# Layer 1's feed-forward on one core: four of its eight chunks as 23 blocks of routed rows

## The chip, the cores and the metric

The kernel is one program on one core of a Trainium2 chip. The metric is device microseconds of one execution: 2776.56 us before, the median of three runs (2775.31 to 2779.29). The profile shown is one further execution of the same program, which took 2766.23 us in all, 2764.4 us of it the span of the trace.

## The reference

Four layers run in sequence over an activation `x` of 4096 tokens (16 samples of 256) by 128 channels. Each has an attention and a feed-forward, each behind a LayerNorm with a shift and scale per sample, and each is added back after a gate per sample:

```
h = layernorm(x) * (1 + ca) + sa;  x = x + ga * attention(h)
h = layernorm(x) * (1 + cb) + sb;  x = x + gb * feedforward(h)
```

In layer 1 the feed-forward holds a second, narrow attention (16 heads of 8 channels), a LayerNorm that makes `x1`, and a mixture of 8 experts of which each token takes two:

```
x1 = ln(h + attention(h))
gates = softmax(x1 @ gW + gb);  w = the two largest gates, the others 0
y[e]  = relu(x1 @ W1[e] + b1[e]) @ W2[e] + b2[e]        128 -> 256 -> 128
ff = ln(x1 + sum over e of w[e] * y[e])
```

All of it is float32. A token's result from the six experts that it does not take is multiplied by zero, so these need not be computed. Layer 0's feed-forward is a similar mixture (top two of 8, with a product of two projections), layer 2 has a narrow causal attention and 16 small experts, layer 3 closes.

## The kernel before

`X` stays in on-chip memory as 32 tiles of 128 tokens; a chunk is 4 tiles, so there are 8 chunks. Every stage is a set of functions, one for each engine (`tensor`, `vector`, `scalar`, `gpsimd`, `sync`), that run over the same numbered steps `t`; the order on an engine is the order in which its function issues. Engines meet at semaphores alone. A stage hosts the last steps of the one before it (`tail`) and the first steps of the next (`guest`), so that stages overlap. There is no planner: the tables of pieces by step are written by hand. Banks of the on-chip accumulators are handed out in rings (`m` 2 banks, `g` 4, `y` 2), and each use waits for the reader of the use before it.

- **Layer 1's mixture** is `moe(1, 8, X1)` (`moe` begins at line 1962). It runs 64 dense units: 8 chunks times 8 experts. A unit of step `t` is `tensor_up` (two products of 128 x 512, float32), ScalarE's two Relu, and, two steps later, `tensor_down` (eight products of 128 x 128) and VectorE's `vector_down` (line 2358): four operations that multiply by the gate and add to the accumulator `ACC`. For each chunk the pieces `x1` (four transposes), `logits`, `gate` (softmax and `keep_top2`), `spread` and `seed` (the bias of the second layer times the gates) stand beside the units. After a chunk's last unit, `gpsimd_finish` and `vector_finish` do the LayerNorm (GpSimd adds `x1`, scales and shifts with `LNW` at lines 2495 and 2497; VectorE subtracts and multiplies at 2383), and the gated residual (lines 171 and 174). The stage's last such finish is hosted by the next stage.
- **Layer 0's mixture** is `routed_experts()` and works otherwise: chunks 0 and 3 are 16 dense units, the six others are routed. VectorE finds the two experts of each token, TensorE ranks them (`rank`), and VectorE makes a row address for each pair of token and expert. GpSimd then writes each tile twice to the array `hs` in device memory by an indirect DMA (line 1853: 48 of them, 128 rows each). Then 31 blocks of 256 rows follow, each with one expert: SyncE reads the row address and the weight address from tables, loads 256 rows (line 1890) and 900 columns of weights (line 1897), TensorE transposes the rows (line 1431), runs the up and down products, and SyncE stores the result in order (line 1902). Weights have four buffers, rows three. In the next stage, wide attention of layer 1, GpSimd gathers each token's two results (line 1209, `late_fetch`) and combines them (`late_combine`).
- **Narrow attention 2** (`narrow_attention(2)`, layer 2) follows layer 1's mixture. It has 128 steps, one for each pair of heads and samples, with a row maximum on VectorE in each (line 3014), and pieces for chunk c from step 16(c - 2) + 2. Its queries and keys go to device memory and back through SyncE (`Parts`, lines 2685 and 2694). It starts as a guest from step 55 of the 64 of layer 1's mixture.
- **Wide attention 0** clears `hs` from device memory, 10 DMAs of 1472 KB on SyncE's queue.

Of the kernel before, what the change touches and what calls it, by code (L numbers as in the profile page):

```python
# [8 lines left out]
F32 = mybir.dt.float32  # L9
F16 = mybir.dt.float16  # L10
BF16 = mybir.dt.bfloat16
# [72 lines left out]
def program(nc, dr, out, stages=STAGES):  # L84
    ctx = ExitStack()
    with ctx:
# [55 lines left out]
        ld_x = [sem(f"ld_x{k}") for k in range(8)]  # L142
# [55 lines left out]
        class Norm:  # L198
# [17 lines left out]
            def stats(self, e, c, i0=0, i1=4):  # L216
                if self.c0 == 0:
                    e.wait_ge(ld_x[c], 16)
                elif i0 == 0:
                    self.arrived(e, c)  # L220
# [61 lines left out]
        def start_up():  # L282
            def sync(e):
                e.dma_start(CT, dr["c0"]).then_inc(ld_wm, 16)
                e.dma_start(WM, dr["wmod0"]).then_inc(ld_wm, 16)
                for k in range(8):
                    e.dma_start(X[:, 4 * k:4 * k + 4, :], dr["x"][:, 4 * k:4 * k + 4, :]).then_inc(ld_x[k], 16)
# [20 lines left out]
        modulation_own = Own(sem("modulation_v"))  # L308

        class Modulation:  # L310
# [3 lines left out]
            def __init__(self, k, sc, gr, tmp):  # L314
                self.k, self.sc, self.gr, self.tmp = k, sc, gr, tmp
                self.own = modulation_own
# [108 lines left out]
        wide_own = Own(sem("wide_v")), Own(sem("wide_g"))  # L425

        def wide_attention(layer, opening=None):
# [14 lines left out]
            own_v, own_g = wide_own  # L442
# [625 lines left out]
            def sync(e):  # L1068
# [4 lines left out]
                for b in range(16):  # L1073
# [13 lines left out]
                    if causal and 2 <= b < 12:  # L1087
                        part = slice(2944 * (b - 2), 2944 * (b - 1))
                        e.dma_start(dr["hs"].rearrange("(p n) c -> p (n c)", p=128)[:, part], dr["zero"]).then_inc(st_zero, 16)
                    if not causal and b == 8:  # L1090
# [50 lines left out]
        moe_own = Own(sem("moe_v")), Own(sem("moe_g"))  # L1141
# [43 lines left out]
        y_stored = [sem(f"y_stored{i}") for i in range(2)]  # L1185
        place(21736)
# [9 lines left out]
        NBLK, SLOT_ROWS = 31, 3072  # L1196

# [14 lines left out]
        def late_combine(e, n):  # L1212

            own, tile = wide_own[1], 8 + n
# [12 lines left out]
        def routed_experts():  # L1227
# [11 lines left out]
            own, own_g = moe_own  # L1239
            scattered, marked, spaced, share_exped = sem("scattered"), sem("marked"), sem("spaced"), sem("share_exped")  # L1240
            placed, table_made = sem("placed"), sem("table_made")
            rows_in = [sem(f"rows_in{i}") for i in range(3)]
            weights_in = [sem(f"weights_in{i}") for i in range(4)]
# [598 lines left out]
            def gpsimd_scatter(e, m):  # L1842
# [3 lines left out]
                if m == 0:  # L1846
                    e.wait_ge(st_zero, 160)
# [113 lines left out]

        def moe(k, E, X1=None):
# [6 lines left out]
            own, own_g = moe_own  # L1969
# [658 lines left out]
        X1A = alloc(4096)  # L2628
# [18 lines left out]
        narrow_own = Own(sem("narrow_v")), Own(sem("narrow_g"))  # L2647
# [93 lines left out]
        def narrow_attention(k):  # L2741
# [9 lines left out]
            own, own_g = narrow_own  # L2751
            causal = k == 2
            X1a = X1A.rearrange("p (t c) -> p t c", c=128)
# [37 lines left out]
            norm = Norm(own, own_g, MODS[k % 2], 2 if k == 1 else 0, slots, r0)  # L2791
# [16 lines left out]
            def hosted_step(i):  # L2808

                if k == 1:  # L2810
# [6 lines left out]
                        [(1, "split"), (1, "v"), (1, "turn")]][i]  # L2817

# [291 lines left out]
            def vector(e):  # L3110
                pads_vector(e, False)
                for t in range(last + 1):
                    if t < 128:
                        rowmax(e, t)
                    if t:
                        for step, b in posts(t - 1):
                            vector_post(e, step, b)
# [1029 lines left out]
```

## Time and profile before

| what | value |
|---|---|
| median of three runs | 2776.56 us |
| the profiled execution | 2766.23 us, its span 2764.4 us |
| TensorE busy | 2608.0 us, 94% |
| VectorE busy | 2017.9 us, 73% |
| ScalarE busy | 1665.9 us, 60% |
| GpSimd busy | 1183.3 us, 43% |
| mean granted TensorE clock | 0.985 |

Times in the rows are microseconds from the span's start. A row of a line in the timeline gives start, duration, engine, line, operation, output and input, the number of operations merged in it, and in brackets how long the engine was idle before it and what ended that. A busy TensorE is not TensorE at its peak: products are pipelined and their ends are modelled. Stages by time: wide attention 0 to about 610, layer 0's mixture to about 880 (its blocks 762 to 855), wide attention 1 to about 1480, narrow attention 1 to 1753, layer 1's mixture to 2012, narrow attention 2 to about 2260, then layers 2 and 3.

### The profile page before, as it was taken

The page shows a single profiled execution, that of the slowest core. Times are in us where ns is not written, and L with a number is a line of the kernel's source. Part 1 is how long each engine was busy: PE and PEld are TensorE (multiplying, and loading weights), DVE is VectorE, ACT ScalarE, POOL GpSimd, SP SyncE. Part 2 cuts the span into 40 slices and gives each one's busy share as a digit, 9 for nine tenths or more (in the row PEclk, how much of TensorE's full clock was granted, in tenths as well). Part 3 has the DMA queues.
Part 4 walks back from the last instruction along what each step waited for, and adds up shares of the span by engine and source line. Part 5 has one row for each costly group of instructions (what it writes and reads, how often), then busy time and mean ns, then how long its engine had stood idle before and what let it go on. Part 6 is the DMA issues. An engine that isn't in the chain of part 4 may idle for free.

```text
span 2764.4 us, 67999 instructions
## 1 busy us (share of the span) xinstructions
PE 2608.0 (94%) x24870; PEld 1786.7 (65%) x24870; DVE 2017.9 (73%) x5620; ACT 1665.9 (60%) x4107; POOL 1183.3 (43%) x1620
## 2 busy tenths in 40 slices
PE   6999999998999999999997999999989989999898
PEld 2666666666687666666664555677767755666676
DVE  6988888876644666676666998466678885887675
ACT  3888888885335766777764777443335544334665
POOL 6888888863602565111124454122333321014441
PEclk9999999999999999999999999999999999999999
DMA  3022221212374111121115543000054433435750
GB/s 114 17 54 76 77 75 48 68 33 82 131 230 129 37 41 42 32 48 32 24 25 145 164 135 122 1 14 3 29 162 140 126 92 63 93 79 158 205 166 28
DMA packets 218857, 230.81 MB, mean 83 GB/s; under 512 B 18608, under 2 KB 188272, under 8 KB 216480
## 3 DMA queue, kind: packets, MB, share of 16 engines
q1 hardware_dynamic: 212000, 207.58, 27.2%
q10 hardware_dynamic: 3456, 12.58, 1.4%
q0 software_dynamic: 3072, 6.30, 0.8%
q8 instruction: 201, 3.29, 0.5%
q14 instruction: 128, 1.05, 0.1%
HBM read 165.87 MB, written 75.60 MB: 87 GB/s over the span
## 4 chain that ended last, share of the span: by engine, by line
PE 73%; DVE 12%; ACT 7%; issue 4%; POOL 2%; DMA 1%; SPq 1%; ACTq 0%; DVEq 0%; POOLq 0%
PE pb L163 65%; ACT big L967 4%; PE pb L663 3%; ACT big L160 2%; DVE big L3014 2%; DVE big L837 2%; PE pb L596 2%; DVE big L236 1%; DVE big L3519 1%; PE pb L2985 1%; PE pb L249 1%; DVE big L820 1%; DVE big L747 1%; POOL hs L1853 1%; DVE big L842 0%
## 5 line engine op out<-in xcount | busy, mean ns | idle before, releaser
L163 PE MATMUL pb<-big 128*128 128x128 f32 (+12 forms) x19624 | 2345.0, 327 | 94.2 <-ACT big L160 32.4
L163 PEld LDWEIGHTS pb<-big 64*128 64x128 bf16 (+4 forms) x19624 | 1476.5, 143 | 750.8 <-issue 422.6
L160 ACT ACTIVATE big<-pb 128x512 f32<-128x512 f32 (+7 forms) x1481 | 846.3, 620 | 541.0 <-PE pb L163 293.0
L160 ACT ACTIVATE big<-pb,big 128x512 f32<-128x512 f32 (+2 forms) x502 | 276.6, 586 | 406.7 <-PE pb L163 356.1
L3014 DVE TENSOR_REDUCE big<-pb 128x4 f32<-128x1024 f32 (+1 forms) x256 | 277.6, 1086 | 71.4 <-PE pb L163 66.8
L967 ACT ACTIVATE big<-big 128x256 f32<-128x256 f32 x512 | 254.0, 499 | 69.5 <-DVE big L842 68.2
L967 ACT ACTIVATE big<-pb,big 128x128 f32<-128x128 f32 (+1 forms) x512 | 257.1, 527 | 60.3 <-DVE big L822 60.1
L837 DVE CUSTOM_DVE_ANT_0 big<-pb,big 128x256 f32<-128x256 f32 x512 | 186.7, 422 | 96.9 <-PE pb L163 96.7
L187 POOL TENSOR_SCALAR big<-big 128x4 f32<-128x4 f32 (+2 forms) x102 | 26.8, 263 | 533.7 <-DVE big L182 533.6
L174 POOL TENSOR_TENSOR big<-big 128x128 f32<-128x128 f32 x168 | 74.8, 459 | 340.8 <-DVE big L171 340.7
L1046 POOL TENSOR_TENSOR big<-big 128x512 f32<-128x512 f32 x128 | 159.9, 1277 | 141.6 <-DMA big<-recip 141.5
L663 PEld LDWEIGHTS pb<-big 64*128 64x128 f32 x3584 | 145.7, 138 | 72.4 <-ACT big L967 55.8
L663 PE MATMUL pb<-big 64*128 64x64 f32 x3584 | 157.7, 225 | 24.0 <-ACT big L967 23.1
L1020 POOL TENSOR_TENSOR big<-big 128x32 f32<-128x32 f32 x32 | 174.1, 5441 | 2.7
L747 DVE TENSOR_TENSOR big<-pb,big 128x512 f32<-128x512 f32 x256 | 163.9, 681 | 13.2 <-PE pb L163 11.7
L904 DVE COPY big<-pb 128x384 f32<-128x384 f32 (+1 forms) x256 | 157.1, 613 | 2.9 <-PE pb L663 1.9
L2358 DVE SCALAR_TENSOR_TENSOR big<-pb,big 128x128 f32<-128x128 f32 x256 | 71.9, 344 | 95.7 <-PE pb L163 95.7
L1011 POOL TENSOR_TENSOR big<-big 128x256 f32<-128x256 f32 x128 | 82.7, 646 | 85.4 <-DVE big L747 82.2
L596 PEld LDWEIGHTS pb<-big 128*128 128x128 f32 x512 | 64.0, 143 | 75.0 <-issue 65.3
L967 ACT ACTIVATION_READ_ACCUMULATOR big<-pb,big 128x1 f32 x512 | 111.3, 217 | 0.0
L236 DVE TENSOR_SCALAR big<-big 128x128 f32<-128x128 f32 x244 | 97.2, 451 | 8.2 <-POOL big L189 8.1
L2737 POOL CAST big<-big 128x16 bf16<-128x16 f32 x96 | 21.9, 228 | 189.1 <-DVE big L3018 73.4
(211 smaller groups left out, 2454.0 us busy)
## 6 DMA issues: line engine op xcount, KB each, us to landing
parts<-big SPq DMA_DIRECT2D x384, 96.0 KB, 2.4
big<-parts SPq DMA_DIRECT2D x72, 512.0 KB, 4.1
big<-recip SPq DMA_DIRECT2D x128, 256.0 KB, 4.9
big<-comb SPq DMA_DIRECT2D x32, 512.0 KB, 8.2
hs<-in_zero SPq DMA_DIRECT2D x10, 1472.0 KB, 8.7
big<-in_wx SPq DMA_DIRECT2D x31, 450.0 KB, 4.4
parts<-big SPq DMA_DIRECT2D x192, 64.0 KB, 2.1
big<-parts ACTq DMA_DIRECT2D x24, 512.0 KB, 4.7
```

What stands on the lines that cost most here:

```text
L160: return e.activation(o, i, f, bias=bias, scale=scale)
L163: return e.matmul(o, l, r_, start=start, stop=stop, skip_group_check=True)
L236: t = e.tensor_scalar(XN[:, i, :], X[:, self.tiles(c)[i], :], mv[:, k0 + i, 0:1], rs[:, k0 + i:k0 + i + 1], ALU.subtract, ALU.mult)
L596: t = e.transpose(bk[:, 128 * m:128 * m + 128], QR[(8 * b + n) % 12][:, 128 * m:128 * m + 128], IDF)
L663: t = e.transpose(banks[2 * (p % 2) + half][:, 64 * at:64 * at + 64], PS[p % 2][rows, i, 128 * blk:128 * blk + 128], IDF[rows, rows])
L747: t = e.tensor_tensor(h3(D), h3(bk), TAB[:, 2 * qk + kk, tile, :].unsqueeze(1).to_broadcast([128, 8, 64]), ALU.mult)
L837: t = e.tensor_tensor_reduce(ps[:, i, x], banks[2 * (p % 2) + i][:, x], U[:, 2 * j + i, 128 - 128 * qt:384 - 128 * qt], 1.0, -3.0e38, ALU. ...
L904: e.tensor_copy(*turned_out(t - 1, 0)).then_inc(even_out, 1)
L967: t = e.activation(ps, banks[2 * s + i][:, at:at + w] if causal else ps, ACT.Exp, bias=NM[s][:, m:m + 1], scale=rstd_q(b)[:, qt, h:h + 1] ...
L1020: e.tensor_tensor(half, half, HALF, ALU.pow).then_inc(rms_made, 1)
L1046: e.tensor_tensor(OT[k % 6], OT[k % 6], R[:, 2 * i:2 * i + 2, :], ALU.mult).then_inc(chunk_scaled, 1)
L3014: e.tensor_reduce(m[:, :, 0:n, jj], two[:, :, 0:width].rearrange("p e (q x) -> p e q x", q=n), AXX, ALU.max, negate=True).then_inc(maxed, 1)
```

## The change

`moe(1, 8, X1)` is replaced by `routed_ffn()`. Chunks 0, 1, 6 and 7 stay dense (units 0 to 15 at steps 0 to 15, units 16 to 31 at steps 39 to 54), chunks 2 to 5 are routed in 23 blocks at steps 16 to 38.

- `X1` gets 130 columns a tile: two more words carry, for each token, the row of its result and the number of its second expert. Routing is done in two groups of two chunks; its pieces stand in the last steps of narrow attention 1 and beside the first 16 units. GpSimd scatters 32 times (128 rows of 520 bytes) into `hs1`, three in a step, at steps 2 to 7 and 8 to 13.
- A block loads 256 rows of `hs1` and 642 columns of weights, has one up product where layer 0 has two, and ends in two indirect DMAs from GpSimd that scatter the results to `ys1` (`SPOT` is their row, worked out by VectorE from the two words).
- A token's two results then lie side by side. SyncE loads them as 8 half chunks (`late_fetch_rows`), and each half (2 tiles) is finished in steps: sum and LayerNorm statistics on VectorE, `late_rstd` on GpSimd, `late_normed` on ScalarE, then scale, shift and gate and the residual. Four halves stand beside the dense units of chunks 6 and 7, scaled and gated by VectorE (`late_scale_vector`); four more, and the four halves of chunks 6 and 7 themselves, stand at steps 8 to 56 of narrow attention 2, with GpSimd doing scale, gate and residual.
- Dense chunks 0 and 1 are finished by VectorE but for the residual. The guest of narrow attention 2 starts at step 48 of 55.
- Wide attention 0 also fills `hs1`: 9 DMAs of 1040 KB. The load of layer 2's second gates moves from block 5 to block 11 of narrow attention 2. Semaphores are shared or renamed (`vector_own`, `gpsimd_own`, `ld_rows`).

```diff
+            DENSE, ROUTED = (0, 1, 6, 7), (2, 3, 4, 5)
+            NB1 = 23
+            T0, T1 = 16, 16 + NB1
+            T = T1 + 16
+            modulated_at, guests_at = T1 + 1, T - 7
+            scatters = {t: [(m, three[m % 3]) for m in range(3 * (t - first), min(3 * (t - first) + 3, 16))]
+                        for first in (2, 8) for t in range(first, first + 6)}
+            summed_at = {T1 + 3: 0, T1 + 4: 1, T1 + 6: 2, T1 + 7: 3}
+            finishes = {10: (0, 1), 12: (0, 2), 13: (0, 3), 18: (1, 1), 20: (1, 2), 21: (1, 3)}
...
+            def tensor_block_up(e, j):
+                s, J = slots["rows", j], NBLK + j
+                e.wait_ge(s.free, s.n)
+                e.wait_ge(weights_in[J % 4], 16 * (J // 4 + 1))
+                s = slots["g", T0 + j]
+                bk = fill(e, s)
+                for f in range(2):
+                    t = mm(e, bk[:, 256 * f:256 * f + 256], WB[J % 4][:, 128 * f:128 * f + 128], HTB[J % 3], True, True)
+                t.then_inc(s.full, 1)
...
+            def vector_block_down(e, j):
+                y, J = slots["y", T0 + j], NBLK + j
+                bk = empty(e, y)
+                if j >= 4:
+                    e.wait_ge(y_placed[j % 4], 32 * (j // 4))
...
+            def scalar(e):
+                for t in range(T + 2):
...
+                        scalar_block_up(e, t - T0)
+                    if T0 <= t + 1 < T1:
+                        scalar_rows(e, t + 1 - T0)
...
+            def gpsimd_block_out(e, j):
+                y = slots["y", T0 + j]
+                e.wait_ge(y.free, y.n)
+                for i in range(2):
+                    e.indirect_dma_start(out=dr["ys1"], out_offset=bass.IndirectOffsetOnAxis(ap=SPOT[j % 4][:, i:i + 1], axis=0),
+                                         in_=YB[j % 4][:, i, :], in_offset=None).then_inc(y_placed[j % 4], 16)
...
+            def sync_weights(e, j):
+                J = NBLK + j
+                if j >= 4:
+                    y = slots["y", T0 + j - 4]
+                    e.wait_ge(y.free, y.n)
...
+        def late_sum(e, i, k):
...
+            for j in range(2):
+                a, n = CHOSEN1[buffer][:, j, :, :], 2 * i + j
+                x = e.scalar_tensor_tensor(out=a[:, 0, :], in0=a[:, k, :], scalar=SHARE1[:, k, n:n + 1],
+                                           in1=a[:, 0, :] if k else X1[:, 8 + n, 0:128], op0=ALU.mult, op1=ALU.add)
...
+                return [(i, t - first) for i, first in zip(range(4, 12), range(8, 56, 6)) if 0 <= t - first < 7]
...
-                 moe(1, 8, X1A.rearrange("p (t c) -> p t c", c=128)), narrow_attention(2), moe(2, 16), layer3_attention(), layer3_mix()]
+                 routed_ffn(), narrow_attention(2), moe(2, 16), layer3_attention(), layer3_mix()]
```

## Rows read from the trace of the kernel before

**Rows 1.** The page: busy time by engine.
```profile
PE 2608.0 (94%) x24870; PEld 1786.7 (65%) x24870; DVE 2017.9 (73%) x5620; ACT 1665.9 (60%) x4107; POOL 1183.3 (43%) x1620
```
**Rows 2.** Busy time by engine in layer 1's mixture; last clock, DMA share, GB/s.
```profile
1753.00:1813.00 60.00, 59.95 (x354) 44.21 (x353) 32.35 (x114) 23.22 (x37) 10.31 (x20) 1.00 0.00 1
```
**Rows 3.** Timeline of VectorE, line 2358, five units in a row.
```profile
1779.94 1.13 DVE L2358 SCALAR_TENSOR_TENSOR big<-pb,big 128x128 f32<-128x128 f32 x4 [2.23 <-PE pb L163]
...
1784.72 1.12 DVE L2358 SCALAR_TENSOR_TENSOR big<-pb,big 128x128 f32<-128x128 f32 x4 [3.01 <-PE pb L163]
...
1788.66 1.13 DVE L2358 SCALAR_TENSOR_TENSOR big<-pb,big 128x128 f32<-128x128 f32 x4 [2.81 <-PE pb L163]
...
1793.06 1.13 DVE L2358 SCALAR_TENSOR_TENSOR big<-pb,big 128x128 f32<-128x128 f32 x4 [2.69 <-PE pb L163]
...
1796.56 1.13 DVE L2358 SCALAR_TENSOR_TENSOR big<-pb,big 128x128 f32<-128x128 f32 x4 [1.18 <-PE pb L163]
```
**Rows 4.** Timeline of one of layer 0's blocks, all engines.
```profile
798.59 0.84 ACT L160 ACTIVATE big<-pb,big 128x256 f32<-128x256 f32 x2 [1.37 <-PE pb L163]
...
799.25 0.38 PE L1431 MATMUL pb<-big 128*128 128x128 f32 x2
...
799.47 2.79 PE L163 MATMUL pb<-big 128*128 128x128 f32 x16
...
799.67 0.39 ACT L160 ACTIVATE big<-pb 128x256 f32<-128x256 f32 x1 [0.24 <-PE pb L1431]
...
800.56 0.42 DVE L1705 TENSOR_TENSOR big<-pb,big 128x256 f32<-128x256 f32 x1 [0.18 <-PE pb L163]
...
801.44 0.35 SPq L1897 DMA_DIRECT2D big<-in_wx  x1
...
802.09 0.38 PE L1431 MATMUL pb<-big 128*128 128x128 f32 x2
```
**Rows 5.** GpSimd's scatter at line 1853: one in the timeline, then all 48 (min/median/max ns).
```profile
739.97 0.96 POOL L1853 DMA_INDIRECT hs<-big  x1 [0.31 <-issue]
...
L1853 POOL DMA_INDIRECT hs<-big x48: 955/962/1248, 683.1 to 755.2; - x48
...
DMA to landing us min/median/max: 2.2/2.2/5.6
```
**Rows 6.** Landing of the 31 weight loads of line 1897.
```profile
DMA to landing us min/median/max: 3.4/4.4/5.8
```
**Rows 7.** Stretches with and without pauses of TensorE; columns as in rows 2.
```profile
795.00:815.00 20.00, 19.73 (x126) 17.71 (x124) 9.95 (x24) 8.59 (x21) 0.00 (x0) 1.00 0.85 236
815.00:820.00 5.00, 2.41 (x11) 1.88 (x12) 1.30 (x3) 0.84 (x2) 0.00 (x0) 0.98 1.11 292
820.00:825.00 5.00, 5.00 (x26) 4.48 (x25) 1.06 (x3) 1.61 (x4) 0.00 (x0) 0.68 0.76 206
615.00:630.00 15.00, 11.88 (x148) 7.90 (x142) 12.59 (x45) 13.42 (x46) 4.36 (x6) 1.00 0.43 95
```
**Rows 8.** VectorE's line 236 without and beside GpSimd's work.
```profile
1973.73 1.11 DVE L236 TENSOR_SCALAR big<-big 128x128 f32<-128x128 f32 x4
...
1988.36 3.91 DVE L236 TENSOR_SCALAR big<-big 128x128 f32<-128x128 f32 x4
```
**Rows 9.** Timeline: narrow attention 2's first split, its reload, and its early scores.
```profile
1990.40 0.61 POOL L2663 CAST big<-big 128x512 bf16<-128x512 f32 x1
...
2000.44 0.81 SPq L2694 DMA_DIRECT2D big<-parts  x2
...
2012.65 0.56 PE L163 MATMUL pb<-big 64*128 64x256 bf16 x8 [1.44 <-DVE big L3014]
```
**Rows 10.** Narrow attention 2, fill and steady part; columns as in rows 2.
```profile
2012.00:2044.00 32.00, 25.47 (x306) 16.70 (x308) 25.92 (x58) 8.60 (x14) 14.40 (x27) 0.79 0.45 153
2044.00:2094.00 50.00, 48.80 (x772) 35.67 (x768) 40.40 (x83) 27.07 (x42) 17.76 (x34) 1.00 0.54 164
```

**Rows 11.** A stretch in which `hs` is cleared; columns as in rows 2.
```profile
300.00:350.00 50.00, 49.38 (x462) 32.21 (x459) 44.07 (x86) 41.80 (x130) 41.16 (x42) 1.00 0.24 79
```

More of the change, by code:

```diff
@@ L217, in stats @@
                 if self.c0 == 0:
[L218 removed]
+                    e.wait_ge(ld_rows[c], 16)
                 elif i0 == 0:
@@ L1238, in routed_experts @@
             T = TD + NBLK
[L1239 to L1243, printed above, removed]
+            own, own_g = vector_own, gpsimd_own
             some = lambda n: [alloc(512) for _ in range(n)]
@@ new lines, in late_stats @@
+        def late_stats(e, i):
+            own, rows = vector_own, late_rows(i)
+            if i >= 8:
+                e.wait_ge(dense_summed[i // 2 - 2].free, dense_summed[i // 2 - 2].n)
+            else:
+                e.wait_ge(own.sem, own.n)
+            if i >= 2:
+                e.wait_ge(ffn_rstd, i - 1)
+            for j in range(2):
+                x = e.bn_stats(LST[i % 2][:, j, :], rows[:, j, :])
+            x.then_inc(own.sem, own.up())
+            e.wait_ge(own.sem, own.n)
+            for j in range(2):
+                x = e.bn_aggr(LMV[i % 2][:, j, :], LST[i % 2][:, j, :])
+            x.then_inc(ffn_mean, 1)
@@ new lines, in late_normed, with late_scale_vector @@
+        def late_normed(e, i):
+            e.wait_ge(ffn_rstd, i + 1)
+            for j in range(2):
+                a = late_rows(i)[:, j, :]
+                x = act(e, a, a, ACT.Identity, LNMR[i % 2][:, j:j + 1], LRS[i % 2][:, j:j + 1])
+            x.then_inc(ffn_normed, 1)
+        def late_scale_vector(e, i):
+            own, a, b = vector_own, late_rows(i), 4 + i
+            two = lambda w: w.unsqueeze(1).to_broadcast([128, 2, 128])
+            e.wait_ge(ffn_normed, i + 1)
+            e.tensor_tensor(a, a, two(LNW[:, 256:384]), ALU.mult).then_inc(own.sem, own.up())
+            e.wait_ge(own.sem, own.n)
+            e.tensor_tensor(a, a, two(LNW[:, 384:512]), ALU.add).then_inc(own.sem, own.up())
+            e.wait_ge(own.sem, own.n)
+            e.tensor_tensor(a, a, two(GA[:, b, 128:256]), ALU.mult).then_inc(ffn_scaled, 1)
@@ new lines, in late_scale @@
+        def late_scale(e, i, part):
+            own, a, b = gpsimd_own, late_rows(i), 4 + i
+            two = lambda w: w.unsqueeze(1).to_broadcast([128, 2, 128])
+            if part == 0:
+                e.wait_ge(ffn_normed, i + 1)
+            elif i < 4:
+                e.wait_ge(ffn_scaled, i + 1)
+            else:
+                e.wait_ge(own.sem, own.n)
+            if part == 3:
+                e.tensor_tensor(X[:, 2 * b:2 * b + 2, :], X[:, 2 * b:2 * b + 2, :], a, ALU.add).then_inc(ffn_added, 1)
+            else:
+                w, op = ((LNW[:, 256:384], ALU.mult), (LNW[:, 384:512], ALU.add), (GA[:, b, 128:256], ALU.mult))[part]
+                e.tensor_tensor(a, a, two(w), op).then_inc(own.sem, own.up())
@@ L3117, in vector @@
                             vector_post(e, step, b)
+                        for i, step in late_at(t - 1):
+                            if step < 2 and i < 8:
+                                late_sum(e, i, step)
+                            elif step == 2:
+                                late_stats(e, i)
                         for b, piece in steps(t - 1):
@@ L3181, in scalar @@
                         scalar_post(e, step, b)
+                    for i, step in late_at(t):
+                        if step == 4:
+                            late_normed(e, i)
                     for b, piece in steps(t):
```

701 lines of the change are left out of this document (676 added, 25 removed).

## The prediction

> **What bounds the kernel now.** I read the page first, for the one engine that is busy nearly throughout: TensorE, 2608.0 us, 94% of the span [rows 1]. Then the busy time by stage, to see whether that holds where the change is made: in layer 1's mixture TensorE is busy 59.95 of 60 us at full clock, VectorE 32.35, ScalarE 23.22, GpSimd 10.31, and the DMA engines move 1 GB/s [rows 2]. So this stage (1753 to 2012, 259 us) lasts as long as its products, and what is taken from TensorE there is gained until another engine or a load becomes the limit. Last the timeline, for the price of a unit and for how a block of layer 0 runs.
>
> **What is removed.** VectorE waits for TensorE before each unit, so its starts give TensorE's pace [rows 3]. A unit with nothing beside it takes 3.50 us (1793.06 to 1796.56). The other gaps hold one piece each: 4.78 for `seed` (1.28), 3.94 for `x1` (0.44), 4.40 for `logits` (0.90); `spread` is four transposes as `x1` is, and I take 0.44 for it too. Together 3.06 a chunk. The stage before is then 64 x 3.50 = 224, seven chunks' pieces 21.4, and 13.6 left for the modulation, the guest and the two closing steps; sum 259.
>
> **What stands in its place.** Three stretches.
>
> 1. Units 0 to 15: 56.0. Beside them stand x1 or its like for four chunks (1.8), logits for four (3.6), spread and seed for chunk 1 (1.7), and two rankings of some ten small products, for which I take 1.0 each as an estimate from the 1.28 of `seed`, which is eight. 65.1 us.
>
> 2. The 23 blocks. Here the limit has to be found, and there are five candidates. (a) TensorE: in rows 4 a block of layer 0 is 2.84 (799.25 to 802.09) with TensorE never idle: 0.22 for the transposes (799.25 to 799.47), 2.62 for six quarter units (four up, two down). The new block has four of the six: 1.75 + 0.22 = 1.97. (b) ScalarE's chain: in layer 0 the second up product (0.87) runs while ScalarE reads the first; now there is none. Both Relu wait for the up products, and the copy of the next rows stands behind them on ScalarE, and the next up product waits for that copy: 0.2 to start, 0.84 for two, 0.39 for the copy, some 0.06 to hand over, then 0.87 for the products [rows 4]: 2.36. (c) The four weight buffers: the load for block j+4 waits until VectorE has emptied block j, and TensorE wants it two blocks after its own end of block j. VectorE starts 0.18 after TensorE and takes 0.42, SyncE issues 0.46 later (800.98 to 801.44) [rows 4], the load lands 3.4 to 4.4 later [rows 6], and is now 71% of the size. Half of 4.5 to 5.5 is 2.25 to 2.75. (d) GpSimd: a scatter is 0.96 and 0.31 before the next [rows 5], two in a block are 2.54. Four result buffers allow GpSimd to fall behind, so that 2.54 sets the pace only in the long run. (e) The DMA engines: in layer 0 they are 85% busy over 2.84 us [rows 7] for 450 + 128 + 128 KB; now 321 + 130 + 128 KB is 82%, so some 2.0. No candidate reaches 2.84, and three lie between 2.3 and 2.75. I take 2.6, as they meet on the same waits: 59.8 us. Beside the blocks stand pieces of 4.8 us on TensorE, which has 0.6 idle a block and hides most, and on VectorE the finish of chunk 1 (steps 18 to 21) and the top two of chunk 7 (step 27), each a few us that delay the emptying on which (c) and (d) hang: 4.0 for both. 63.8 us; bounds 54 (2.36 and nothing beside it) and 71 (2.84 and six).
>
> 3. Units 16 to 31: 56.0 and the same 13.6 as before: 69.6.
>
> The sum is 198.5 against 259: 60.5 us less.
>
> **What it costs elsewhere.** The last steps of narrow attention 1 get two more turns and logits (2.7 us of TensorE, which has pauses there) and routing on VectorE: +2, bounds 0 and 4. At the first block, 32 scatters at 1.27 with two small jobs leave GpSimd about 2 us behind its three a step; a landing of 2.2 [rows 5] and the load of rows, which I take to land like a weight load, 4.4 [rows 6], follow: +1.5, bounds 0 and 5. In units 18 to 25 VectorE has 1.13 for the unit and about 4.0 for a half (four sums at the 0.28 of rows 3, four small statistics that I put at 0.28 too, three scalings of 128 x 256 at the 0.42 of line 1705 in rows 4, and hand-overs), in 3.50 us: it is full, but the sums begin three units after the last block, when results have landed (two scatters 2.5, landing 2.2, load 4.4). +2, bounds 0 and 6. The guest starts two units nearer the end. Its first split stands 22.2 us ahead of the scores, of which 14.5 are the trip of queries and keys through device memory (10.0 to the reload's issue, and a landing that I take at 4.4 again), so two units (7.0) just fit: 0 to 2, and against it VectorE no longer has the last finish (about 5 us) in the fill of narrow attention 2, where TensorE is busy 25.47 of 32 us and waits for VectorE [rows 9, 10]: together 0, bounds -4 and +2. In the steady part VectorE has 9.6 free of 50 us [rows 10]; eight halves add about 2.5 us each for four and 1.1 each for four within 80 us, and GpSimd's part, four operations of 128 x 256 that I put at 0.61 each [rows 9] and a root, 3 to 4 each, stands beside 17.76 of 50: +2, bounds 0 and 6. Moving the load of second gates and renaming semaphores: nothing, since neither is waited for. The nine fills of `hs1` are like the clearing of `hs`, beside which TensorE is busy 49.38 of 50 us [rows 11]: 0, bounds 0 and 2. Sum +7.5.
>
> So -53 us. The profiled execution, 2766.2 (span 2764.4), becomes 2713; the median of the runs lies 10.3 above it, and I carry the difference over to it: 2776.6 - 53 = **2723.5**.
>
> **Two rules weighed.** Line 236 takes 1.11 us alone and 3.91 beside GpSimd's operations [rows 8], while the 48 scatters keep 955 to 1248 ns, median 962, with VectorE at work beside them [rows 5]. The Trainium skill ("SBUF — State Buffer", section "Who interferes with whom") has VectorE's two-port modes and GpSimd exclude each other, and its section "SBUF: two separate sides" has a scatter's descriptors starved for as long as VectorE holds the ports. By that rule, the trace agrees on line 236 and shows little of the starving. It is rival B's sharper form.
>
> TensorE's clock fell to its lower level (1.2 of 2.4 GHz) after it had stood for 2.5 us in 815 to 820: 0.68 in the next 5 us; with pauses that leave it 79% busy over 15 us it stayed at 1.00 [rows 7]. The Trainium skill ("TensorE: Matmul & The Clock Gate", "HAM oscillation — how this bites in real kernels") warns that a loop whose every pass waits for a load falls back each time. By that rule the blocks would run as in rival C.
>
> **Rivals.**
> - *B, GpSimd's scatter is the bound and slower than alone.* Its longest is 1.25, with 0.31 between: 3.1 a block, 71.8 for 23, with the 4 beside it 76: +12, 2735. For it: two scatters in each block for the first time, with stores and loads beside them. Against: the median of 48 is 0.96 [rows 5].
> - *C, the clock.* TensorE is idle a quarter of each block. At the lower level 1.97 becomes 3.94: 90.6 for 23 and 4 beside it, +31: 2754. For it: 76% is under the 79% of rows 7. Against: the pauses are 0.6 us, a quarter of the one that cost it.
> - *D, slower than before: the weight loop.* If loads that share the queue with scattered rows land late, (c) grows: period = (1.1 + landing) / 2. The saving of 53 is used up when a block takes 2.6 + 53 / 23 = 4.9, at a landing of 8.7 us; at 10 us it is 5.55, +68: 2791. For it: the DMA engines are the nearest to full here. Against: the longest of 31 larger loads was 5.8 [rows 6].
> - *E, the late halves do not hide.* All of VectorE's added work in narrow attention 2 (about 14 us) and 6 in the units lands on the path: +16, 2740. Against: VectorE has 9.6 free of 50.
>
> **Chances.** The forecast 0.70, B 0.10, C 0.10, E 0.07, D 0.03. The forecast's own bounds run from -71 (blocks at 54, nothing elsewhere but 0) to -35: 2706 to 2742; B and E lie inside, C and D are left out. Range 2705 to 2745. A measurement of this kernel can't tell less than 0.2% (5.6 us) from no change: faster 0.97, same 0.01, slower 0.02.
>
> **What would show it.** In the profile after: 23 blocks at 2.4 to 2.8 us (transposes at the new rows' line), ScalarE's copy straight behind two Relu, GpSimd two scatters a block without pause; the stage from first unit to first scores near 200 us; clock 1.00 through the blocks; narrow attention 2 longer by under 6 us. Wrong: blocks above 3 us, a clock of 0.5 in them, a stop of over 5 us before the first block or behind the last, or narrow attention 2 longer by 10.

## The result, and the profile after

The changed kernel takes 2745.86 us (median of 4 runs, 2736.33 to 2755.77), the kernel before 2777.35 beside it: ratio 0.9887, interval 0.9851 to 0.9923. A second time: 2741.52 against 2776.97, 0.9867 [0.9842, 0.9892]. So the change gains 31 to 35 us where 53 were forecast. The time lies just above the range of 2705 to 2745; the second one lies inside it. What has to be explained is the 18 to 22 us of gain that did not come.

The page of the profiled execution (span 2744.9), the row that answers to [rows 1]:
```profile
PE 2552.5 (93%) x24523; PEld 1747.5 (64%) x24523; DVE 1983.2 (72%) x5568; ACT 1653.1 (60%) x4133; POOL 1245.7 (45%) x1692
```
TensorE is busy 55.5 us less, near the 60.5 forecast for the stage (a rough figure, since some records of products can be missing). The span of this trace is only 19.5 us shorter, and the median 31 to 35.

Now by stage, columns as in [rows 2]: units 0 to 15, the blocks, units 16 to 31. Each stretch runs from a mark on VectorE (the first sum of a unit, the first emptying of a block) to the next.
```profile
1779.77:1851.11 71.34, 62.31 (x375) 46.95 (x375) 38.63 (x167) 21.54 (x39) 35.22 (x42) 0.98 0.18 58
1852.28:1922.00 69.72, 58.13 (x349) 48.32 (x348) 22.02 (x78) 27.85 (x70) 45.43 (x48) 0.95 0.58 165
1927.30:1984.00 56.70, 53.68 (x330) 41.20 (x330) 42.62 (x154) 22.15 (x38) 17.79 (x32) 1.00 0.30 93
```
In the first two TensorE stands still for 9 and 11.6 us, and no engine beside it is full. What the engines wait for, from the table of waits in 1760 to 1935 (total, times, longest us):
```profile
ACT big L160 <- remote: 29.8, 9, 9.4
DVE big L2507 <- remote: 16.0, 4, 5.7
DVE big L2495 <- remote: 12.6, 3, 5.4
...
POOL hs L2648 <- remote: 4.1, 2, 2.3
```
"Remote" means that no local instruction ended when the engine woke, and there is one core. The timeline shows one such place, TensorE's products, VectorE's sums of a unit, ScalarE's Relu and GpSimd's scatter:
```profile
1799.34 10.28 PE L163 MATMUL pb<-big 128*128 128x512 f32 x53
...
1798.84 1.13 DVE L2507 SCALAR_TENSOR_TENSOR big<-pb,big 128x128 f32<-128x128 f32 x4 [0.30 <-PE pb L163]
1807.15 1.13 DVE L2507 SCALAR_TENSOR_TENSOR big<-pb,big 128x128 f32<-128x128 f32 x4 [5.54 <-remote]
...
1802.12 0.69 ACT L160 ACTIVATE big<-pb,big 128x512 f32<-128x512 f32 x1 [0.77 <-PE pb L163]
1812.18 2.42 ACT L160 ACTIVATE big<-pb,big 128x512 f32<-128x512 f32 x4 [9.38 <-remote]
...
1802.89 0.96 POOL L2648 DMA_INDIRECT hs<-big  x1 [0.31 <-issue]
1804.15 0.95 POOL L2648 DMA_INDIRECT hs<-big  x1 [0.30 <-issue]
1805.41 0.96 POOL L2648 DMA_INDIRECT hs<-big  x1 [0.30 <-issue]
```
The trace also records when a semaphore is updated, that is, when the engines that wait for it are told. Set beside the ends of TensorE's products (own reading of these records):
```
product for   its end    the update   late by
VectorE       1803.01    1807.13      4.12
VectorE       1804.09    1812.11      8.02
ScalarE       1805.15    1812.16      7.01
ScalarE       1806.01    1812.20      6.19
VectorE       1807.79    1812.36      4.57
```
The consumers start 0.02 us behind the update, so they do wait for it. The ends of products are modelled, but their starts are recorded, and TensorE went on starting products, 53 of them in the 10.28 us of the row above, while the news of the earlier ones was outstanding. In this trace 102 of TensorE's updates are over 0.3 us late, all in stretches in which GpSimd issues indirect DMAs; in the trace of the kernel before there is none, though it has 48 scatters and 48 gathers. I call them late updates. Such counts depend on how products and updates are paired where records are missing (strictly one to one it is 82 here); what holds by either way is none against many. Only TensorE's updates are late: of those of VectorE, ScalarE and GpSimd in the same trace, some 5000, none is over 0.3 us behind. Late updates stand in layer 0 too, whose code is the same. There, in 680 to 770, before and after:
```profile
680.00:770.00 90.00, 87.37 (x464) 59.52 (x464) 54.53 (x204) 30.25 (x51) 52.82 (x62) 0.98 0.40 134
```
```profile
680.00:770.00 90.00, 81.66 (x403) 52.88 (x403) 51.13 (x197) 28.15 (x46) 52.60 (x62) 0.96 0.31 104
```
Narrow attention 1's last row maximum comes at 1747.3, before 1732.3: 15 us are lost ahead of the changed stage. The first block waits for its rows, as TensorE's transposes of them show:
```profile
1841.01 0.44 PE L2245 MATMUL pb<-big 128*128 128x128 f32 x2 [4.02 <-DMA big<-hs]
```
The block's emptying (line 2497) and narrow attention 2's row maxima (line 3830), by the view of one line with first and last start:
```profile
L2497 DVE TENSOR_TENSOR big<-pb,big x23: 414/419/421, 1852.3 to 1919.5; 128x256 f32<-128x256 f32 x23
...
L3830 DVE TENSOR_REDUCE big<-pb x128: 924/958/962, 1984.3 to 2271.1; 128x6 f32<-128x768 f32 x128
```
A block takes (1919.5 - 1852.3) / 22 = 3.05 us; from the first sum of a unit to the first score the stage takes 204.5 (before 250.8), narrow attention 2 286.8 from its first to its last row maximum (before 279.2).

### The profile page after: what moved, and what is told of

Read it like the earlier page. It is cut to its first block, busy times and chain, and to the rows that moved or that the text cites. A ratio compares the mean times of both kernels' runs of the same rounds, so it can differ in the third digit from the quotient of the medians.

```text
span 2744.9 us, 67535 instructions
## 1 busy us (share of the span) xinstructions
PE 2552.5 (93%) x24523; PEld 1747.5 (64%) x24523; DVE 1983.2 (72%) x5568; ACT 1653.1 (60%) x4133; POOL 1245.7 (45%) x1692
## 4 chain that ended last, share of the span: by engine, by line
PE 65%; DVE 13%; ACT 7%; issue 5%; POOL 4%; DMA 2%; SPq 2%; another core or an unknown queue 1%; ACTq 0%; DVEq 0%; POOLq 0%
PE pb L163 56%; ACT big L966 4%; PE pb L662 3%; ACT big L160 3%; DVE big L3830 2%; SPq L3489 2%; DVE big L836 2%; PE pb L595 2%; DVE big L236 1%; DVE big L4352 1%; PE pb L3801 1%; PE pb L249 1%; POOL hs L1866 1%; DVE big L179 1%
## 5 line engine op out<-in xcount | busy, mean ns | idle before, releaser
L163 PE MATMUL pb<-big 64*128 64x256 bf16 (+13 forms) x19247 | 2284.6, 326 | 115.4 <-ACT big L160 42.7
L163 PEld LDWEIGHTS pb<-big 64*128 64x128 bf16 (+5 forms) x19247 | 1431.1, 142 | 750.9 <-issue 410.9
L160 ACT ACTIVATE big<-pb,big 128x256 f32<-128x256 f32 (+2 forms) x484 | 249.6, 560 | 378.3 <-PE pb L163 285.7
L174 POOL TENSOR_TENSOR big<-big 128x128 f32<-128x128 f32 x136 | 60.8, 458 | 320.1 <-DVE big L171 319.9
L966 ACT ACTIVATION_READ_ACCUMULATOR big<-big 128x1 f32 x512 | 96.1, 188 | 0.0
```

What stands on the lines that cost most here:

```text
L160: return e.activation(o, i, f, bias=bias, scale=scale)
L163: return e.matmul(o, l, r_, start=start, stop=stop, skip_group_check=True)
L966: t = e.activation(ps, banks[2 * s + i][:, at:at + w] if causal else ps, ACT.Exp, bias=NM[s][:, m:m + 1], scale=rstd_q(b)[:, qt, h:h + 1] ...
```

## The experiments

Four questions: where do the 15 us come from, what makes units 0 to 15 and the blocks slow, what is a block's own pace, and why is narrow attention 2 longer.

**1. Where the 15 us come from.** The changed kernel again:

> The changed kernel once more, nothing altered. In its first trace TensorE's semaphore updates come 1 to 6 us late while GpSimd's indirect DMAs run, already in layer 0, whose code is the same, and the last row maximum of narrow attention 1 stands at 1747.4 against 1732.3 before. Theory 'the program' (its semaphores or its memory cause it): it comes again, narrow attention 1 ends 12 to 18 us later than in the kernel before, time 2736 to 2756. Theory 'the execution' (this one execution was disturbed): the 15 us are gone, narrow attention 1 ends within 2 us of the kernel before, time about 2731.

Measured: 2741.52; row maximum at 1744.5, 108 late updates. "The program" held against one disturbed execution of the changed kernel. Then the kernel before with those parts of the change that reach beyond its stage. Bookkeeping alone (a cut of the edit):
```
-        wide_own = Own(sem("wide_v")), Own(sem("wide_g"))
+        vector_own, gpsimd_own = Own(sem("vector_own")), Own(sem("gpsimd_own"))
+        (every semaphore at its number in the changed kernel)
```


> The kernel before with only the bookkeeping of the semaphores as in the change: one counter for VectorE's own hand-overs and one for GpSimd's through the whole program, every semaphore at the number it has in the changed kernel. Theory 'semaphores': layer 0's scatters and wide attention 1 lose the same 12 to 18 us, 2790 to 2795, and late updates of TensorE appear beside the scatters. Theories 'memory' and 'the execution': 2777 within 4 us, no late update.

Memory alone (shortened):
```
+  dr["hs1"], dr["ys1"] = ...   # two tensors in device memory
+  e.dma_start(dr["hs1"]...[:, part], dr["blank"][:, part]).then_inc(st_zero, 16)   # nine times
```


> The kernel before with only the memory side of the change: the two new tensors in device memory and the nine fills of hs1 in wide attention 0, and the wait for them before the first scatter. Theory 'memory': 2790 to 2795, with late updates of TensorE beside layer 0's scatters. Theories 'semaphores' and 'the execution': 2777 to 2780 (the fills themselves 0 to 2), no late update.

And the changed kernel with the old numbers:

> The changed kernel with every semaphore that the kernel before has too at the number it had there (scattered 222 for 194, the gathers' 193 and 194 for 190 and 191), the ten new ones on the numbers left. Theory 'semaphores', in its form that the numbers matter: the 15 us of layer 0 come back and part of the stage of the blocks with them, 2715 to 2732. In its form that the shared counters matter, and by the theories 'memory' and 'the execution': as the changed kernel, 2736 to 2756.

Measured: 2776.69 (ratio 1.0001 [0.9988, 1.0014]), 2776.52 (0.9998 [0.9983, 1.0012]), and 2741.6 for the last. Both copies of the kernel before have late updates in their traces (43 and 38), and 13 and 11 of the 15 us at narrow attention 1's last row maximum, and still the usual time of the kernel before. Each theory had tied late updates to a longer time, and the usual time to none. If the copies are like the kernel before, its usual time contains them. So it was profiled again, unchanged:

> The kernel before, nothing altered, profiled once more. Its first trace (2766.2, 10 us under the median of its runs) has no late semaphore update of TensorE; two near copies of it, at their median of 2777, have 41 and 45 over 0.3 us beside layer 0's scatters and wide attention 1's gathers. Theory 'usual': the late updates belong to this kernel too and its first trace was an unusual execution: about 40 again, first row maximum of narrow attention 1 at 1500 to 1504. Theory 'copies': the copies brought them in: none, 1490.

(The two counts in that text are 43 and 38, as above.) Measured: 2783.6, 57 late updates, narrow attention 1 from 1501.5. Its row in 680 to 770:
```profile
680.00:770.00 90.00, 81.75 (x415) 53.36 (x414) 49.71 (x180) 27.82 (x46) 52.78 (x62) 0.98 0.35 116
```
81.75 as in the changed kernel, not 87.37. "Usual" held: the trace that the prediction rests on was an unusually good execution, 10.3 us under the median, and all three other traces of this kernel and its near copies have late updates.

**2. What the late updates are and cost.** Indirect DMAs replaced, one group at a time (the edits told in short; each kernel leaves out the placing of what it writes, so its output is not the layer's):
```
 plain results:    46 scatters of results -> SyncE: e.dma_start(dr["ys1"][256 * j + 128 * i:...], YB[j % 4][:, i, :])
 plain both:       and 32 scatters of rows -> GpSimd: e.dma_start(dr["hs1"][128 * i:...], X1[:, 8 + 8 * g + t, :])
 before, plain rows: layer 0's 48 scatters -> SyncE: e.dma_start(dr["hs"][128 * m:...], HN[i][...])
 strided rows:     plain results; rows still indirect, index 8 * p + const instead of the routed one
```


> The changed kernel with the 46 scatters of the block results replaced by 46 plain stores of SyncE in block order (the result is then in the wrong places: this leaves out their return to the tokens). Theory L (late updates: TensorE's semaphore updates are held back while GpSimd issues indirect DMAs one behind the other): no late update behind the last scatter of rows at about 1835, a block takes 2.4 to 2.6 us instead of 3.06, 11 to 15 us less: 2727 to 2731. Theory S (the blocks' own waits, ScalarE's chain or the weight buffers, set 3.06): 2740 to 2745. Theory M (the DMA engines are too full): as S, or slower.

> As the kernel with plain stores of the results, and the 32 scatters of rows too are plain DMAs of GpSimd (it leaves out the sorting by expert: the blocks read blank rows). Theory L in the form that GpSimd's own DMAs with an index are what holds TensorE's updates back: units 0 to 15 take 65 to 67 us instead of 74.8, 2717 to 2722. In the form that any DMA of GpSimd's queue does it: as the kernel with plain results alone, within 3 us. Theory C (what else stands beside the units, rankings and tables on VectorE, makes them 74.8): no gain either.

> The kernel before with layer 0's 48 scatters of rows replaced by plain stores of SyncE (it leaves out the sorting by expert in layer 0); the 48 gathers of wide attention 1 stay. Theory L: the scatters cost the kernel before 6 to 9 us in most executions, so 2767 to 2771. If the late updates cost nothing on the path: 2777 within 3 us.

> The kernel with plain stores of the results, and the 32 scatters of rows go by a regular index, every eighth row, instead of the routed one (it leaves out the sorting by expert). Theory G (the indirect DMA itself, as GpSimd issues it, holds TensorE's updates back): units 0 to 15 with late updates as before, 70 to 73 us from first to last, about 2731. Theory A (the addresses, scattered over device memory, do it): no late updates in 1775 to 1845, 61 to 63 us, about 2722.

| kernel | median | unit 0 to first block | block | stage | late updates in the stage |
|---|---|---|---|---|---|
| changed | 2745.9, 2741.5 | 72.5 | 3.05 | 204.5 | 58 |
| plain results | 2731.8 | 71.7 | 2.72 | 197.1 | 26 |
| strided rows | 2737.2 | 72.1 | 2.70 | 197.0 | 22 |
| plain both | 2724.2 | 62.4 | 2.74 | 187.7 | 0 |

Theory L held in each, in its form of the indexed DMA: plain results gained 7.5 us of the stage (11 to 15 expected of the whole, 10 to 14 measured), plain both 9.4 more. A plain DMA of GpSimd in the same place is harmless, a regular index is not: it is the indirect DMA, not the queue and not the addresses. Its figures were hit less well than its direction: a block was expected at 2.4 to 2.6 and takes 2.72, plain both at 2717 to 2722 and takes 2724.2, strided rows at about 2731 and take 2737.2 (two runs). The kernel before with plain rows takes 2766.0 (0.9957 [0.994, 0.9973]; 2767 to 2771 expected); the late updates left in its trace stand beside the gathers. Its row, and the units of the kernel with plain both:
```profile
680.00:770.00 90.00, 88.56 (x480) 61.35 (x479) 55.33 (x206) 30.35 (x51) 6.09 (x14) 0.98 0.41 135
```
```profile
1769.70:1830.90 61.20, 59.12 (x375) 45.46 (x375) 38.69 (x167) 22.31 (x39) 21.83 (x41) 1.00 0.21 66
```
The same 375 matmuls in 61.2 us instead of 71.34. No wait for "remote" is left there in 1760 to 1935.

**3. A block's own pace.** On the kernel with plain both:
```
+                    if T0 <= t < T1 - 1:
+                        tensor_rows(e, t + 1 - T0)      # now ahead of tensor_block_up; the same on ScalarE
```


> The kernel with plain DMAs for rows and results, in which a block takes 2.74 us without late updates; here the transposes and the copy of the next block's rows stand ahead of the block's up products and Relu on TensorE and ScalarE. Theory B (ScalarE's chain sets the pace: up products, two Relu, copy, next up products, one behind the other): a block takes 2.0 to 2.3 us, 10 to 16 us less than 2724. Theory K (the loop through the four weight buffers sets it): 2.6 to 2.75, no gain beyond 3 us.

A second run has the same edit, and only its first four blocks load weights (TensorE's wait for them goes with the loads):
```
-                    if j + 4 < NB1:
-                        sync_weights(e, j + 4)
```


> The kernel with plain DMAs and the rows ahead of the up products (2.70 us a block), and only the first four blocks load their weights; the other nineteen use what lies in the buffers (it leaves out their weights). Theory K (the loop through the four weight buffers sets the pace): a block takes 2.0 to 2.2 us, what TensorE's own work needs, and the time is 11 to 15 us less. If GpSimd, VectorE's emptying or the rows' loads set the pace: 2.6 to 2.75.

Measured: 2721.1 with 2.70 a block, and 2717.1 with 2.24:
```profile
L2499 DVE TENSOR_TENSOR big<-pb,big x23: 417/419/422, 1843.9 to 1903.4; 128x256 f32<-128x256 f32 x23
```
```profile
L2500 DVE TENSOR_TENSOR big<-pb,big x23: 418/419/423, 1844.2 to 1893.4; 128x256 f32<-128x256 f32 x23
```
Theory B fell. K's pace nearly came (2.0 to 2.2 expected). Of the 11 to 15 us that were expected with it, the stage is 9.8 shorter in the trace (177.2 against 187.0), and the medians, of two runs each, differ by 4. At 2.24 the blocks are bound by TensorE's products:
```profile
1844.20:1896.00 51.80, 50.76 (x349) 45.71 (x348) 22.17 (x81) 29.96 (x70) 2.37 (x3) 1.00 0.39 106
```
But K is not shown, for there is a rival that I had not named. SyncE's queue in the first of the two:
```profile
1869.66 0.34 SPq L2709 DMA_DIRECT2D big<-in_wx  x1
1870.49 0.39 SPq L2695 DMA_DIRECT2D big<-hs  x1
1870.94 0.93 SPq L2701 DMA_DIRECT2D ys<-big  x2
1872.36 0.34 SPq L2709 DMA_DIRECT2D big<-in_wx  x1
1873.20 0.39 SPq L2695 DMA_DIRECT2D big<-hs  x1
```
From issue to issue 2.70 us, the block's pace, and what lies between are the register loads for the next address (0.28 each): SyncE never rests. Weights 0.84, rows 0.88, and 0.99 for the two plain stores that my own experiment had moved there. So 2.72 to 2.74 is the pace of these experiments, not of the change, in which SyncE has 1.7 a block. Between late updates the changed kernel shows its own (second trace; transposes at the new rows' line):
```profile
1876.23 0.38 PE L2245 MATMUL pb<-big 128*128 128x128 f32 x2
...
1878.57 0.38 PE L2245 MATMUL pb<-big 128*128 128x128 f32 x2
...
1880.90 0.27 PE L2245 MATMUL pb<-big 128*128 128x128 f32 x1
```
2.34 and 2.33: what the forecast had for ScalarE's chain (2.36). TensorE is busy 4.49 of these 4.67 us, though, so its own work is nearly as long. Two periods of one trace are little, and what the blocks would take in the changed kernel without late updates is not shown.

**4. Narrow attention 2.**

```
-                if not causal or t < 8:
+                if not causal or t < 1000:      # no late half; the waits for them go too
```


> The changed kernel with the eight late halves of narrow attention 2 left out: their sums, norms, scalings and additions (the output misses them). Theory E (they do not hide): narrow attention 2 takes 279 us from first to last row maximum as in the kernel before, instead of 289: 2731 to 2735. Theory N (narrow attention 2 is longer for another reason, its start or the transfers): 286 to 290, 2738 to 2743.

Measured: 2734.0; 275.2 instead of 286.8 to 289.9, theory E. By stretches of scores (first row maximum of each):

| kernel | 0-8 | 8-24 | 24-64 | 64-112 | 112-127 | all |
|---|---|---|---|---|---|---|
| before | 16.0 | 33.1 | 83.2 | 108.1 | 38.8 | 279.2 |
| changed | 12.8 | 35.5 | 90.2 | 108.1 | 40.2 | 286.8 |
| late halves out | 12.0 | 33.1 | 83.2 | 108.1 | 38.8 | 275.2 |
| late later | 13.0 | 35.4 | 89.2 | 108.1 | 36.7 | 282.3 |
| short sums | 12.8 | 33.5 | 92.7 | 108.1 | 39.1 | 286.2 |
| short scalings | 13.0 | 34.6 | 92.4 | 108.1 | 40.2 | 288.3 |
| every 8 | 13.0 | 33.6 | 86.0 | 109.5 | 40.0 | 282.1 |

The stretch from 112 to 127 varies by itself, from 37.9 to 41.4 in the other traces of the kernel before and its near copies, so the last column is a weaker measure than that of scores 24 to 64. In plain both, which has no late update in its stage, scores 24 to 64 take 90.2 too: what is lost there is not theirs.

The last four rows are attempts to find the price of a late half:
```
 late later:      ScalarE's norm at step 5 (was 4), GpSimd's root at 4 (3), its scalings at 6 and 7 (5, 6)
 short sums:      late_sum over 8 of 128 columns for halves 4 to 11
 short scalings:  late_scale over 8 of 128 columns for halves 4 to 11
 every 8:         zip(range(4, 12), range(8, 72, 8))      # was range(8, 56, 6)
```


> The changed kernel, with the late halves of narrow attention 2 a score later on two engines: GpSimd's root, ScalarE's normalization and GpSimd's scalings stand one score further from VectorE's sum. In the change they cost narrow attention 2 about 12 us between scores 20 and 64. Theory W (waits between engines: VectorE's part runs one score behind, GpSimd and ScalarE stand at its statistics with the attention's work queued behind them): the wait of ScalarE for GpSimd's root (10 us, five times) goes, narrow attention 2 takes 280 to 284 us instead of 289, 2733 to 2738. Theory V (VectorE itself is full, lengthened by GpSimd beside it): 287 to 290, 2739 to 2744.

> The changed kernel with the sums of the four late halves of narrow attention 2 over 8 of 128 columns: the same instructions and waits, but 16 of them some 0.3 us shorter (it leaves out the rest of the sums). From score 24 to score 64 the change takes 90 to 93 us, the kernel before 83.4. Theory V (VectorE is full, its busy time counts): 85 to 87. Theory P (GpSimd's work beside VectorE stretches VectorE, or stands in front of the splits): 89 to 92. Theory W' (hand-overs count, not work): 89 to 92 too.

> The changed kernel with GpSimd's scalings and additions of the eight late halves over 8 of 128 columns: the same instructions and waits, but 32 of them some 0.5 us shorter (it leaves out the rest). Theory P: from score 24 to score 64 in 84 to 87 us. Theories V and W': 89 to 92.

> The changed kernel, complete; the eight late halves of narrow attention 2 start every 8 scores instead of every 6, from score 8 on, so that ScalarE's normalization always stands 4 scores into a group, never behind a split of GpSimd. In the change single scores at 23, 33 and 57 are 1.5 to 3.4 us longer than in the kernel before, others not at all. Theory W'' (the in-order queues of ScalarE and GpSimd: a late half hurts only where its root stands behind a split): scores 24 to 64 in 83 to 86 us instead of 90 to 93, narrow attention 2 in 278 to 282, 2732 to 2737. Theory H (each half costs about 1.2 us of hand-overs wherever it stands): 89 to 92 for these scores and 2738 to 2743.

Measured: 2742.3, 2740.1, 2749.2 and 2734.6 (0.9841 [0.9822, 0.9859]). V and P fell: less work on either engine took nothing from scores 24 to 64. W in its first form failed as well: its 280 to 284 came (282.3), but by scores 112 to 127; ScalarE's wait for GpSimd's root, which should have gone, is still 6.9 us in 4, scores 24 to 64 take 89.2, and the time is V's and not W's. The lost time is not spread; it stands in single scores, 23, 33, 51 and 57, each 0.9 to 2.1 us longer (up to 3.6 in the second trace). Score 33 of the changed kernel, by its timeline:
```profile
2047.20 0.87 POOL L174 TENSOR_TENSOR big<-big 128x128 f32<-128x128 f32 x2 [6.43 <-DVE big L171]
...
2049.50 0.20 POOL L2035 TENSOR_TENSOR big<-big 128x2 f32<-128x2 f32 x1
...
2049.73 0.88 ACT L160 ACTIVATE big<-big 128x128 f32<-128x128 f32 x2 [2.71 <-POOL big L2035]
...
2051.63 2.55 PE L163 MATMUL pb<-big 64*128 64x256 bf16 x48 [1.71 <-ACT big L160]
...
2053.67 0.96 DVE L3830 TENSOR_REDUCE big<-pb 128x6 f32<-128x768 f32 x1 [2.42 <-PE pb L163]
```
GpSimd waits 6.43 us for VectorE with the attention's own work at its head; the late half's root stands behind that; ScalarE has reached the late normalization and waits 2.71 for the root, with the copies for TensorE behind it. "Late later" moved the long scores (to 25, 40 and 52) and kept them. "Every 8", which puts the normalization at the same harmless place in each group of eight scores, took 4 of the 7 us. Of the waits of ScalarE in 2030 to 2115 the changed kernel has this one, and "every 8" no such row:
```profile
ACT big L160 <- POOL big L2035: 9.7, 5, 2.7
```
Theory W'' held (83 to 86 expected, 86.0 measured); 1.4 came back in scores 64 to 112, where the last half now stands.

**The best version.** Last, in the complete kernel, the rows ahead together with each way of moving the late halves:

> The changed kernel, complete, with both edits: late halves a score later, and rows ahead of the up products. Theories W and B together, with late updates still in the way of the blocks: 2724 to 2732. If the late updates set the blocks' pace alone: as the kernel with late halves later, 2733 to 2738. Theories V and K: 2738 to 2743.

> The same, and in the blocks the transposes and the copy of the next rows stand ahead of the up products. With late updates and the weight loop setting the blocks' pace, the second edit gives 0 to 2 us: 2731 to 2737 by theory W'', 2737 to 2743 by theory H. Were ScalarE's chain a limit beside them, 5 us or more under the kernel with the first edit alone.

Measured: 2739.9 (0.9869 [0.985, 0.9887]) and 2737.6 (0.9847 [0.9833, 0.9864]). Rows ahead gains nothing. "Every 8" alone is the best at 2734.6; its interval overlaps the changed kernel's, so that it is faster than the kernel before is shown, and faster than the changed kernel only likely.

## Why the prediction missed, step by step

**The frame.** "The median of the runs lies 10.3 above it, and I carry the difference over to it." As a number this held: against a usual trace of the kernel before (the one with the fills, at its median) what lies ahead of the stage is 3.9 longer, and 1.1 in the second trace of the change. But the 10.3 were not an offset of the measurement. Of the 12.0 us between the spans of the two traces, 11.1 stand ahead of narrow attention 1's last row maximum, where the usual one has late updates beside 48 scatters and 48 gathers; without layer 0's scatters the kernel before is 11 us faster. So the base was a trace in which the price of an indirect DMA can't be seen, and the change adds 78 of them. From this trace to the changed kernel's, +15 us stand ahead of the stage.

**The stage: here is the step that failed.** The 78 indirect DMAs were priced by GpSimd's time, by the landing of rows and by VectorE's ports; that they hold back the engines that wait for TensorE had no term. Together with the first block's stop they cost 16.8 us of this stage (204.5 against 187.7), where the forecast had 1.5. Its three terms, carried over to marks that a trace has (a unit's sum stands two steps behind its start, a block's emptying one): from the first sum to the first emptying 65.1 - 7.0 + 2.6 + 1.5 = 62.2; from there to the first sum of unit 16, 22 blocks, two units and the 4.0 for disturbances, 68.2; from there to the first score the rest of the forecast's 250.8 - 57 = 193.8, 63.4.

| | forecast | changed | plain both |
|---|---|---|---|
| units 0 to 15 | 62.2 | 72.5 | 62.4 |
| blocks | 68.2 | 75.0 | 66.9 |
| units 16 to 31 | 63.4 | 57.0 | 58.4 |
| sum | 193.8 | 204.5 | 187.7 |

"Plain both" has no indirect DMA in this stage, but its blocks run at the 2.74 of SyncE's queue. Had they 2.33, the 16.8 would be more by up to 9, and so would the work that the forecast sized too high; no run settles this.

*Units 0 to 15 and the first block's 1.5*: the work was sized right, 62.4 without indirect DMAs. With them it is 10.1 more. Of that, 3.3 is TensorE's stop for the first block's rows (the row with 4.02 above; 4.0 in the second trace too, 0.7 in plain both), for which the forecast had 1.5 with bounds 0 and 5. The rest lies on TensorE's hand-overs and was in no term.

*Blocks, 2.6 each*: measured 3.05, between late updates 2.33. None of the candidates (a) to (e) sets 3.05. Candidate (a), TensorE's own work, had 1.97 and some 0.2 for the pieces beside; where TensorE is the limit (no loads) a block takes 2.24. Rival B named the place (the result scatters) and nearly the pace (3.1), by luck, for its reason is not there: line 2655's scatters take 952 to 1347 ns, median 958. Rival C, a lower clock throughout, fell: the mean is 0.95. But the mean hides two falls to the lower level, each after a stop of TensorE (2.3 and 3.0 us), and together they took up to 3.4 us:
```profile
1865.00:1870.00 5.00, 2.66 (x16) 2.24 (x16) 0.71 (x3) 1.71 (x4) 4.20 (x5) 0.96 0.67 199
1870.00:1875.00 5.00, 5.00 (x27) 4.47 (x27) 1.13 (x5) 1.11 (x3) 3.52 (x4) 0.70 0.49 145
...
1885.00:1890.00 5.00, 3.25 (x12) 2.54 (x13) 2.71 (x8) 0.49 (x2) 3.70 (x4) 0.66 0.67 192
```
D's loads land in 2.8 to 5.4 us, median 3.1, in the kernel with plain both; far from its 8.7.

*Units 16 to 31, and VectorE full +2*: 5 to 6 too high. The +2 is not seen.

**Narrow attention 1's tail: +2.** Measured 3.9 (from the last row maximum to the first sum 32.5, before 28.6), within its bounds.

**Narrow attention 2.** Start and fill 0, bounds -4 and +2: -3.2 in scores 0 to 8 (VectorE without the last finish, as argued). Steady part +2, bounds 0 to 6: +9.4 in scores 8 to 64 and, in the second trace, +12.4. Mis-sized: I had counted busy time, and most of it is a wait in ScalarE's queue. Rival E ("the late halves do not hide") came true here in size: with them narrow attention 2 takes 286.8 to 289.9, without them 275.2. It did not in its reason, VectorE's added work, for shorter sums gave nothing back.

**Bookkeeping and fills: nothing.** Right: 1.0001 and 0.9998.

**The sum.** Against the usual trace: +3.9 ahead, +3.9 for the tail, -46.4 for the stage, +7.9 for narrow attention 2, -0.8 behind it: -31.5, span against span (2744.9 and 2776.4). Forecast: +2 - 57 + 2 = -53. Of the 21.5 between them the indirect DMAs of the stage are 16.8, narrow attention 2 5.9, the tail 1.9, what lies ahead and behind 3.1, less 6.1 by which the forecast for the stage lies above plain both.

**The range.** Its upper end, -35, is not the sum of the terms' own bounds: all of them at once (7.2 for the blocks, 25 elsewhere) give -60.5 + 7.2 + 25 = -28, a time of 2748, and both measurements lie below it. The prediction does not say how it came to -35.

**The rules weighed.** Indirect DMAs keep their 958 ns in the blocks, so the row speaks against starved descriptors here as it did before. The Trainium skill ("SBUF — State Buffer", "Who interferes with whom") states that "DMA never contends with a compute engine"; taken as "a DMA costs the engines nothing", it would have made the stage 187.7 with the scatters as without, and it is 204.5. What is held back, though, is not TensorE's work but the news of it, and on that the rule says nothing.

## What to carry to other kernels

Before a trace is used as the base of a sum, ask why its time is not the median's: a difference of 10 us has a place, and a change can double what stands there. Price a GpSimd indirect DMA not only by its own time but by what it does to engines that wait for TensorE, here 0.2 to 0.3 us each beside dense products (16.8 us for 78, 11 for 48, 10.1 for 32). And when work is slipped into in-order queues, look for what stands behind it and at which phase of the loop; shortening it may gain nothing where moving it does.

## What the runs showed of the hardware

While GpSimd issues indirect DMAs, TensorE's semaphore updates come up to 8 us late, and those of the other engines do not. Of the 20 traces 19 show it, all but the first of the kernel before. The products run on until a buffer is missing. The updates then come in a row, 0.04 us apart. Plain DMAs from the same engine (32 of 537 ns) do not do it. In such stretches the trace also misses landing records: it holds 362 of layer 0's 768 in the changed kernel, where the good trace has all. What in the chip holds them, and why one execution was free of it, was not found; nor was pacing the scatters tried.
